# First pass of a Hartley-spectrum kernel: 64-column tiles for two of its products, and another order of them

## What is computed

```
def dht_2d(x):
    f = jnp.fft.fftn(x, axes=axes)
    ff = jnp.fft.fftn(x[..., ::-1, ::-1], axes=axes)
    result = f.real - ff.imag
    norm = jnp.sqrt(jnp.sum(result * result, axis=axes, keepdims=True))
    return jnp.where(norm != 0, result / safe, 0.0)
...
    x_ht = dht_2d(x)
    out_modes = compl_mul2d(x_ht[:, :, :M1, :M2], weights1)
    out_ht = out_ht.at[:, :, :M1, :M2].set(out_modes)
    return idht_2d(out_ht)
...
    x = x + _L0_conv_ref(_gn(x), L0_conv_weights1)
    x = x + _L1_conv_ref(_gn(x))
    return x
```

## Time and profile before

| | us |
|---|---|
| median of 3 runs | 2905.59 (2889.78 to 2907.07) |
| profiled execution | 2896.12 |
| its span, first to last instruction | 2894.3 |
| TensorE busy / VectorE / ScalarE / GpSimd in the span | 2736.1 / 2073.9 / 2096.0 / 911.3 |
| first pass | about 24 to 985 of the span |

### The profile page before, as it was taken

One profiled execution on the slowest core, in us unless ns is written; L12 is line 12 of the kernel. 1 busy time (PEld: TensorE's weight loads), 2 busy tenths in 40 slices (PEclk: granted clock), 3 DMA queues, 4 the chain that ended last, 5 costly groups with the idle time before them and its releaser, 6 DMA issues.

```text
span 2894.3 us, 51534 instructions
## 1 busy us (share of the span) xinstructions
PE 2736.1 (95%) x16764; PEld 2151.0 (74%) x16764; DVE 2073.9 (72%) x2783; ACT 2096.0 (72%) x3633; POOL 911.3 (31%) x533
## 2 busy tenths in 40 slices
PE   6999999999999666899999999999999999999998
PEld 6989889898899666566666666666666666666666
DVE  5767666676777534677877777877777877877777
ACT  5767666576667323578878878878878878888887
POOL 2323233232333302233333333333333333333332
PEclk9999898898999677899999999999999999999999
DMA  6545454454555324155555555555555555555554
GB/s 188 156 133 150 132 146 132 131 155 131 152 144 148 76 62 105 44 150 164 162 152 165 160 150 165 160 156 161 161 153 166 158 152 165 160 153 163 165 167 124
DMA packets 808870, 421.14 MB, mean 146 GB/s; under 512 B 20912, under 2 KB 807344, under 8 KB 807472
## 3 DMA queue, kind: packets, MB, share of 16 engines
q1 hardware_dynamic: 808624, 417.86, 50.7%
HBM read 283.56 MB, written 134.22 MB: 144 GB/s over the span
## 4 chain that ended last, share of the span: by engine, by line
PE 49%; ACT 5%; DVE 3%; issue 3%; DVEq 0%; ACTq 0%
PE g_ps L963 37%; PE y_ps L949 6%; PE v_ps L937 5%; ACT grad L1026 3%; ACT g_ps L1019 2%; DVE coef_t L1063 1%; DVE grad L1075 1%; PE v_ps L925 1%; ACT u_hi L1004 0%; ACT grad L1017 0%; ACT v_sb L1010 0%; DVE xbuf L1100 0%; DVE xbuf L1070 0%; DVE coef L1106 0%; DVEq L1100 0%
## 5 line engine op out<-in xcount | busy, mean ns | idle before, releaser
L963 PE MATMUL g_ps<-u_hi,stencil 128*128 128x512 f32 x2560 | 1054.7, 412 | 1.9 <-DVE grad L1075 1.9
L963 PE MATMUL g_ps<-u_lo,stencil 128*128 128x512 f32 x2560 | 1018.6, 398 | 0.0
L905 POOL TENSOR_TENSOR u_lo<-xbuf,u_hi 128x1024 fp32r<-128x1024 f32 x256 | 565.6, 2209 | 1139.9 <-ACT u_hi L1004 1133.8
L963 PEld LDWEIGHTS g_ps<-u_hi,stencil 128*128 128x128 f32 x2560 | 484.2, 189 | 305.6 <-issue 188.9
L1100 DVE SCALAR_TENSOR_TENSOR xbuf<-xbuf,rows,grad 128x256 f32<-128x256 f32 x1024 | 575.7, 602 | 153.0 <-ACT grad L1026 152.8
L332 PEld LDWEIGHTS t_ps<-first_sb,xbuf 128*128 128x128 f32 x4096 | 525.1, 201 | 68.8 <-issue 42.5
L963 PEld LDWEIGHTS g_ps<-u_lo,stencil 128*128 128x128 f32 x2560 | 482.5, 188 | 103.0
L332 PE MATMUL t_ps<-first_sb,xbuf 128*128 128x64 f32 x4096 | 512.4, 281 | 39.9 <-DMA second_sb<-second 23.5
L1026 ACT ACTIVATE grad<-grad,eps,rows 128x256 f32<-128x256 f32 x1024 | 530.5, 595 | 0.1
L1017 ACT ACTIVATE grad<-g_ps 128x512 f32<-128x512 f32 x512 | 302.2, 590 | 293.1 <-PE g_ps L963 293.0
L1075 DVE TENSOR_TENSOR grad<-grad,g_ps 128x512 f32<-128x512 f32 x512 | 352.0, 687 | 224.6 <-ACT g_ps L1019 218.0
(11 more groups left out here) (116 smaller groups left out, 2383.3 us busy)
## 6 DMA issues: line engine op xcount, KB each, us to landing
xbuf<-x SPq DMA_DIRECT2D x256, 512.0 KB, 5.1
xbuf<-x SPq DMA_DIRECT2D x512, 256.0 KB, 3.0
out<-xbuf SPq DMA_DIRECT2D x512, 256.0 KB, 2.7
xbuf<-weights SPq DMA_DIRECT2D x8, 800.0 KB, 11.2
wmix<-weights SPq DMA_DIRECT2D x8, 800.0 KB, 13.8
second_sb<-second SPq DMA_DIRECT2D x1, 1230.0 KB, 8.4
mats_sb<-mats SPq DMA_DIRECT2D x1, 704.0 KB, 6.5
first_sb<-first SPq DMA_DIRECT2D x1, 32.0 KB, 6.4
```

What stands on the lines that cost most here:

```text
L905: nc.gpsimd.tensor_tensor(u_lo[:, r % 2, :, 1:W + 1], x_of(xbuf, r), u_hi[:, r % 2, :, 1:W + 1].bitcast(FP32), ALU.subtract)\
L963: mm = nc.tensor.matmul(g_ps[h][:, axis], stencil[:, m, :], u[:, r % 2, 4 * h:4 * h + 4, o:o + W], start=n == 0, stop=n == len(todo) - 1)
```

## The change

The first and the second axis are issued as two matmuls with 64 weight columns each, in place of one with 128. Columns 0 to 63 of the weights write partitions 0 to 63 of the output, columns 64 to 127 write partitions 64 to 127. The two alternate. The mirrors and the edges keep their form. The order on TensorE changes: a chunk's two halves of the first axis come first, then the second axis of the tile before, then the mirrors of both halves. The waits stay at the pieces to which they belonged. The other engines' programs are not touched.

```diff
@@ -305,10 +305,12 @@
                         skip = a - (2 * j - 1)
-                        mm = nc.tensor.matmul(
-                            r_ps[bank][:, (a - edge * bank) * MODES:(b - edge * bank) * MODES],
-                            tmodes[:, par, t, :], second[:, t, skip * MODES:(skip + b - a) * MODES],
-                            start=t == (0, SPLIT)[bank], stop=t == NB - 1, skip_group_check=True)
+                        for c in range(2):
+                            side = slice(64 * c, 64 * (c + 1))
+                            mm = nc.tensor.matmul(
+                                r_ps[bank][side, (a - edge * bank) * MODES:(b - edge * bank) * MODES],
+                                tmodes[:, par, t, side], second[:, t, skip * MODES:(skip + b - a) * MODES],
+                                start=t == (0, SPLIT)[bank], stop=t == NB - 1, skip_group_check=True)
...
@@ -321,28 +323,36 @@
+            def first_axis(i, k, g):
+
+                pe.wait_ge(first_out, i * HALVES + 2 * k + g + 1)
+                for p in range(HALF):
+                    for c in range(2):
+                        side = slice(64 * c, 64 * (c + 1))
+                        mm = nc.tensor.matmul(t_ps[g][side, p, :], xbuf[:, k % SLOTS, HALF * g + p, side], first[:],
+                                              start=True, stop=True)
+                mm.then_inc(pe_first, 1)
+
+            def mirror(i, k, g):
+
+                pe.wait_ge(mirrored, i * HALVES + 2 * k + g + 1)
+                pe.wait_ge(lo_ready, i * HALVES + 2 * k + g + 1)
+                for n, part in enumerate((x_hi, x_lo)):
+                    nc.tensor.matmul(z_ps[g][:], flips[:, 0, :], part[:, g, :, 2:66],
+                                     start=n == 0, stop=False)
+                    mm = nc.tensor.matmul(z_ps[g][:], flips[:, 1, :], part[:, g, :, 0:64],
+                                          start=False, stop=n == 1)
+                mm.then_inc(pe_mirror, 1)
+
             def tile(i, par):
                 for k in range(CHUNKS):
...
+                    pe.wait_ge(x_in[k % SLOTS], arrived(i, k))
+                    first_axis(i, k, 0)
+                    first_axis(i, k, 1)
+                    if not is_first(i) and k < CHUNKS - 1:
+                        second_axis(i - 1, 1 - par, k)
+                    mirror(i, k, 0)
+                    mirror(i, k, 1)
                     if k == 1 and not is_first(i):
                         edges(i - 1, 1 - par)
```

More of the change, by code:

```diff
@@ L324, in tile @@
             def tile(i, par):
                 for k in range(CHUNKS):
[L326 to L345, removed]
```

## The result

| | us |
|---|---|
| changed kernel, median of 4 runs | 2676.38 (2672.72 to 2678.87) |
| kernel before beside it, median of 4 runs | 2904.1 (2889.78 to 2907.07) |
| ratio | 0.922, 95% interval 0.919 to 0.925 |
| forecast | 2802 (2740 to 2965) |
| span of the profiled execution | 2670.9, before 2894.3 |

The direction was right; the size was not.

A forecast was written before the change was run, and what follows sets the result against it. TensorE, paying for 128-column loads, was taken to bound the first pass; savings of 63 and 5 us on chunks, 22 at low clock and 8.5 on the last tile, together 98.5, gave 2802 us, range 2740 to 2965.

The forecast's parts named there:

- Issue: Handing matmul pairs (one load, one matmul) to TensorE: 0.057 us each for long, taken from the mixing stage; 16 to 18 queued.
- the term of 2.31 us: TensorE's 56.6 pairs after ScalarE's copy: 32 in 0.91 us from the queue, 24.6 more at 0.057 in 1.40.
- ScalarE's link: From a mirror's end through ScalarE's high part, square and copy of t_ps: 2.91 us, 3.0 with the handover.
- my 6.2: Forecast time in us of a first-pass chunk with second axis, against 6.84 before.
- VectorE's 5.1 us per chunk: VectorE's busy time per first-pass chunk; a chunk without second axis was therefore put at 5.25 us, not 4.8.
- The last tile: Its second axis, standing alone: 172 pairs at 0.057, 9.8 us instead of 18.3, saving 8.5 us.
- Changes of shape: Loads idle when TensorE switches between half-array and full products: two per chunk, 0.38 us together.
- The copy of t_ps becomes the next wait: TensorE waits for ScalarE's copy before half 1's first axis, some 0.7 us per chunk.
- The low clock: Stretches at clock 0.50 after loop turns keep their 110 us, hold 3.7 chunks more and save 22 us.
- nothing limits issue: Rival, chance 0.12: the mixing's 0.057 belongs to its single tile; chunk 5.5 us, time 2729 to 2740 us.
- no overlap: Rival, chance 0.25: column halves load one after the other; chunk +0.5 us, time 2961 us.
- The gain was not given back: Rival, chance 0.10: overlap holds but changes of shape cost 0.4 to 0.5 us each; 2880 to 2910 us.

The follow-up runs named there:

- run 3: Changed kernel with all matmuls of columns 0 to 63 first, then all of 64 to 127, instead of alternating: 2822.9 us, ratio 0.973.
- run 7: Changed kernel plus rows of throwaway matmuls behind the first pass; per pair 0.113 us at 128 columns, 64 columns 0.058 in one tile, 0.029 in two.
- run 4: Changed kernel with column halves kept but the old order (mirrors after each half's first axis): 2663.8 us, ratio 0.917.
- Run 5: Changed kernel with ScalarE's copy of t_ps put ahead of its square: 2662.2 us, ratio 0.916.
- run 9: VectorE sums squares over half the columns: changed kernel 2669.4 us; with ScalarE's copy first and TensorE's loop written out as well, 2588.2 us.
- run 1: Changed kernel with both axes back at 128 columns, only the new order kept: 2882.8 us, ratio 0.995.
- run 6: Changed kernel with TensorE's own loop over tiles in the first pass written out: 2634.4 us, ratio 0.907.

## Why the prediction was wrong

**What bounds the kernel, and the mechanism: right.** TensorE set the first pass, paid for 128-column loads and not for columns streamed, and two column halves in turn load and stream side by side (runs 3 and 7). Of the Trainium skill's two rules, "TensorEngine Tiling (Array Packing)", Key Properties, agrees with the trace. That of "TensorE: Matmul & The Clock Gate", Part 3, that a load overlaps matmuls only where the row group differs, does not hold here: both tiles use all 128 rows, and 192 pairs take as long as 96 in one tile, 5.68 and 5.67 us. One reading was loose: only a call of the two axes is recorded as two loads and two matmuls; a mirror's call is one of each. The counts in the sum are right.

**The step that failed is "Issue".** I took 0.057 us as the rate at which pairs can be handed to TensorE, since the mixing stage has it at both clocks. The inference was that a cost independent of the array's clock must be one of handing over. A third cause was open, and I did not look at it: how the operands lie in memory. Run 7 shows 0.032 for the same form with contiguous operands, and 0.0084 for four tiles in turn. In the chunk's chain this is the term of 2.31 us for the pairs behind ScalarE's copy. It has nothing at 0.057 in it: from the load of 307.86 to the mirror's load of 309.64 are 1.78 us, of which 0.19 are the change of shape, so 56 pairs took 1.6 us, 0.028 each. With the mirrors behind them, from the load of 307.86 to the last mirror product of half 0, at 310.45, are 2.59 us, where my terms gave 3.21.

**ScalarE's link was 0.3 us too long.** I measured 2.91 us from the mirror to the end of the copy, in the earlier trace rows. But before, the copy waited there for the first axis itself: the square that starts at 940.92 with 1.04 us is over at 941.96, the copy starts at 942.05. Where ScalarE is free to go on, in the changed kernel, the copy starts 0.10 us before the square's record ends, so 0.2 of the 0.3 us are this wait. In the changed kernel the same link, from 305.17 to the load at 307.86, is 2.69, against 3.0. A link must be measured where its own steps touch each other. Both terms together, 0.62 + 0.31, are the 0.93 us between my 6.2 and the 5.29 of the trace.

**What that makes.** A chunk with second axis gained 1.55 us instead of 0.64. One without gained 0.9 instead of 0.25: 5.5 to 4.6 (all 15 such chunks behind the first tile at clock 1.00 take 4.6). By my own counts (98 and 21.5 chunks) that is 171 us and not 68, 103 of the 126 us by which the forecast missed. VectorE's 5.1 us per chunk, which I took for a floor there, bounds the mean of the chunks and not a single one: its work is the same 5.0 us in a chunk of 4.6 us, and it can catch up in those of 5.3.

**The last tile** was forecast at 9.8 us and took 7.25. For half of it the forecast was nearly right: there the clock is 0.50 and the loads come in couples 0.107 us apart, 0.053 per pair, where I had 0.057. Then the clock rises to 1.00 and a pair costs 0.029; before, the whole last tile ran at 0.50. **Changes of shape**, 0.19 each: right (0.15 to 0.2 in run 4 and in the trace), but the idle time of the loads lies elsewhere: 0.38 us before the first axis, and 0.06 to 0.07 before a chunk's first mirror, where I had named 0.2. **The copy of t_ps becomes the next wait**: right in kind and place; 0.4 us where I said 0.7. Run 5 takes most of it away and run 9 shows who comes next.

**The low clock.** I kept the length of the stretches after the turns. They shrank: 0.06 x 933 x 2 = 110 us of the pass before, 0.03 x 721 x 2 = 43 us after. More than half of this is the new order, which alone leaves 73 (run 1). The stops themselves did not shrink: at a turn they went from 2.9 to 4.8 us in all to two of together 7. What the pass gained beyond chunks and last tile is 222 - 171 - 11 = 40 us (the pass ends at 763 us and not at 985), against the 22 that I gave it. These 18 us more, with the 103 of the chunks and 2.5 of the last tile, make 124 of the 126. Why the stretches are shorter was not tested; run 6 shows that without stops the stage's mean clock is 0.99.

```profile
24.00:714.00 690.00, 659.32 (x12050) 543.30 (x12049) 635.97 (x706) 582.13 (x956) 306.01 (x256) 0.99 0.70 191
```

**The rivals.** The nearest was "nothing limits issue", which I gave 0.12. That nothing limits issue is what happened, though the single tile, which it blames for the 0.057, is not the reason (run 7: 0.032 in a single tile). But its 2729 to 2740 us stood on the same too long link and the same floor of 5.1 us, so it missed as well, and with it the lower end of my range. The rival that ends slower, no overlap, is refuted by run 7, where two tiles in turn take 0.029 us per pair and one tile 0.058, and by run 3: the same instructions in blocks are 146 us slower. The gain was not given back.

## What to carry to other kernels

Where fp32 weights of 128 rows are loaded for few moving columns (64 here), the load is the price, and two matmuls of half the weight columns in turn cost half of it (0.058 us against 0.113); put next to each other the ones that go to different column halves. Before a rate from another stage is taken as a limit, its operands' layout has to be compared as well as its shapes. And a chain that a faster engine uncovers has to be timed from links that do not already wait for that engine. When two parts of a change are tried one by one, each has to be compared with the kernel that has everything else of the change.

## What the runs showed that I had not expected

- Strided operands (1280 bytes from column to column) raise a pair of 32 columns from 0.032 to 0.056 or 0.057 us on either side and to 0.072 on both.
- Two column tiles overlap at the border of two blocks even where the program does not alternate: loads of the next tile start while some of the tile before are still to come, and the mean pair fell from 0.058 to 0.050 us.
- The stops at a turn of TensorE's loop grew with the change, from 2.9 to 4.8 us in all to two of together 7. The new order alone already has two at each turn, of 1.8 to 2.2 and 2.3 to 2.9 us. Whether the rest comes of a body that runs faster or of one with more instructions, no run separates. Writing out the loop of one engine alone was worth 1.6%.
- The order of a loop's body changes how long the clock stays low behind a turn: 73 us of the pass in run 1 against 110 before, with the same matmuls.
